# Expert results of a fused attention and mixture-of-experts kernel: scattered to their tokens as they come, and read back by plain loads

## What is computed

```python
x = L0_attn_x                                  # (2, 1024, 256): 2048 tokens of width 256
xn = layernorm(x)
# attention: (2, 1024, 256) seen as tokens of width 16, windows of 8 positions,
# softmax, a 3-tap convolution, projection, a norm over 16; result: "attention"
topk_idx, topk_weight = gate(xn)               # 6 of 16 experts for each token
out = 0
for e in range(16):
    inter = silu(xn @ gate_proj[e].T) * (xn @ up_proj[e].T)      # width 176
    out = out + comb[:, e:e+1] * (inter @ down_proj[e].T)        # comb: weight of e, or 0
shared = (silu(xn @ sg.T) * (xn @ su.T)) @ sd.T                  # width 352
return x + attention + out + shared
```

## Time and profile before

| what | us |
|---|---|
| three runs | 451.7, 457.14, 457.64 |
| median | 457.14 |
| the profiled execution, its time | 456.78 |
| its span, first to last instruction | 455.0 |

### The profile page before, as it was taken

The page is one execution under the profiler, slowest core; times in us unless marked ns, Lnnn a source line. Parts: engine busy times, 40 slices in busy tenths (PEclk is TensorE's granted clock), DMA queues, the critical chain, the costliest instruction groups (busy, mean ns, idle before and its releaser), DMA issues.

```text
span 455.0 us, 7300 instructions
## 1 busy us (share of the span) xinstructions
PE 400.8 (88%) x1989; PEld 310.2 (68%) x1989; DVE 364.8 (80%) x593; ACT 224.8 (49%) x616; POOL 234.7 (52%) x221
## 2 busy tenths in 40 slices
PE   7799599999999999997999999989989999999200
PEld 7688499889767677675777777767667777767200
DVE  2869953686899989999799999999995355479951
ACT  3654234325564445653476864675437744554200
POOL 3530156775777777873000000007787777778671
PEclk9889979999999999999899999999999999999755
DMA  7998422226455766576733334336657997665652
GB/s 169 330 412 354 163 107 88 98 76 223 132 184 190 205 207 197 184 229 184 216 114 103 97 95 121 103 90 169 196 166 202 287 234 194 175 198 160 201 151 81
DMA packets 55878, 80.55 MB, mean 177 GB/s; under 512 B 8480, under 2 KB 47264, under 8 KB 55584
## 3 DMA queue, kind: packets, MB, share of 16 engines
q1 hardware_dynamic: 42912, 50.91, 36.7%
q0 software_dynamic: 9216, 25.96, 18.8%
q10 hardware_dynamic: 3712, 3.21, 2.4%
HBM read 43.48 MB, written 36.57 MB: 176 GB/s over the span
## 4 chain that ended last, share of the span: by engine, by line
PE 49%; DVE 22%; issue 12%; DMA 5%; POOL 4%; ACT 2%; SPq 2%; ACTq 1%; DVEq 1%; POOLq 0%
PE gate L991 15%; PE ps_y L1014 10%; POOL xs_dram L594 4%; PE ps_y L942 4%; DVE prod L1094 4%; DVE qkv L1094 4%; PE up L920 3%; PE ps_y L1007 3%; DVE inter_s L1532 3%; PE up L981 3%; DVE sc L1094 2%; PE gate L920 2%; DVE yacc L1614 2%; PE misc L882 2%; PE misc L1041 2%
## 5 line engine op out<-in xcount | busy, mean ns | idle before, releaser
L991 PE MATMUL gate<-wrec,xgT 128*128 x444 | 151.3, 463 | 2.9 <-ACT xgT L725 1.8
L594 POOL DMA_INDIRECT xs_dram<-xrow,slot_i x96 | 111.4, 1160 | 50.6 <-DMA xs_dram<-xrow,slot_i 21.5
L1014 PE MATMUL ps_y<-wrec,interT 88*128 x444 | 115.2, 382 | 0.0
L614 POOL DMA_INDIRECT gat<-y_dram,slot_i x50 | 55.0, 1099 | 113.6 <-DMA y_dram<-y_s 98.9
L991 PEld LDWEIGHTS gate<-wrec,xgT 128*128 128x128 f32 x444 | 75.8, 190 | 28.2 <-issue 4.4
L1014 PEld LDWEIGHTS ps_y<-wrec,interT 88*128 88x128 f32 x444 | 76.0, 191 | 6.7 <-issue 0.3
L1532 DVE SCALAR_TENSOR_TENSOR inter_s<-gate,xg,gate_s 128x176 f32<-128x176 f32 x111 | 43.6, 393 | 33.8 <-ACT gate_s L733 32.9
L733 ACT ACTIVATE gate_s<-gate 128x176 f32<-128x176 f32 x111 | 35.2, 317 | 70.1 <-PE ps_y L1007 67.7
L753 ACT ACTIVATE y_s<-ps_y 128x256 f32<-128x256 f32 x107 | 41.0, 383 | 55.7 <-PE up L981 52.6
L1007 PEld LDWEIGHTS ps_y<-ident,inter_s 128*88 128x88 f32 x222 | 26.7, 123 | 37.6 <-issue 19.3
L1007 PE MATMUL ps_y<-ident,inter_s 128*88 128x128 f32 x222 | 42.7, 274 | 5.0 <-DVE y_s L1556 2.8
(11 more groups left out here) (215 smaller groups left out, 633.8 us busy)
## 6 DMA issues: line engine op xcount, KB each, us to landing
xg<-xs_dram SPq DMA_DIRECT2D x111, 136.0 KB, 2.6
y_dram<-y_s SPq DMA_DIRECT2D x111, 128.0 KB, 2.1
wrec<-wexp SPq DMA_DIRECT2D x14, 608.0 KB, 15.1
xs_dram<-zrow SPq DMA_DIRECT2D x1, 2176.0 KB, 13.0
xn_dram<-xrow SPq DMA_DIRECT2D x8, 256.0 KB
qkv<-xn_dram SPq DMA_DIRECT2D x8, 256.0 KB
xs_dram<-xrow,slot_i POOLq DMA_INDIRECT x96, 2.9
wrec<-wexp SPq DMA_DIRECT2D x1, 1216.0 KB, 5.6
```

The source lines that it names most:

```text
L594: nc.gpsimd.indirect_dma_start(xs_dram[0:DONE[max(d for d in DONE if d <= c)] * P, :], bass.IndirectOffsetOnAxis(slot_i[:, o:o + 1], 0), x ...
L614: nc.gpsimd.indirect_dma_start(places[place_of(n)][:, there:there + H], None, y_dram[0:DONE[max(d for d in DONE if d <= first)] * P, :], b ...
L991: last = nc.tensor.matmul(guA[t % 2][:, 0:2 * I], xgT[:, t % 2, k * P:(k + 1) * P], wrec[:, bass.ds(record + k * 2 * I, 2 * I)], start=(k ...
L1014: last = nc.tensor.matmul(ps_y[:, t % 2 * 2 * H:t % 2 * 2 * H + H], interT[:, t % 2, k * P:(k + 1) * P], wrec[0:HALF, bass.ds(record + KT ...
```

## The change

The gathers of the combine go; each tile's result rows are scattered to their tokens instead.

- Each dispatched row is 16 values wider (`XW` = 288): for each expert, the number of the row in `y_home` (2048 tokens x 6) that the product with that expert belongs to, token times 6 plus its rank among the six. `routing` computes it with two more VectorE operations. Rows of zero padding carry `NOWHERE` = 1e6 there.
- ScalarE copies, in each round, one column of the tile's table (the tile's expert) to `home_i` as integers (`home_rows`).
- SP stores the results of tiles 0 to 106 to `y_dram` as before, and loads each back to one of six buffers `y_back` in round max(38 + 5s//8, s + 4) (`load_back`); first it waits for the store and for the scatter that used the buffer before.
- POOL, after the dispatch, scatters tile s from there (tiles 107 to 110 directly from `y_s`) to `y_home`: 111 indirect DMAs, with a bounds check that drops the padding rows; for tile s it waits for `mid_ok` of at least 38 + 5s//8.
- SP loads fetch n from `y_home` with one plain DMA (rows of 1 KB, 6 KB apart), in rounds 84 to 90 one each, 91 to 101 three in two rounds, 104 to 106 two each, and the last twelve after the loop, at the head of its output stores; five places instead of seven. VectorE adds fetches 0 to 29 two rounds after their loads, 30 and 31 between the last steps of `normalise`, the rest at the end.
- `XN_AT` goes from 87 to 95 and `PACED` from 40 to 36. Some tables change places in SBUF.

```diff
-XW = H + NE
+XW = H + 2 * NE
+NOWHERE = 1e6
...
-PACED = 40
+PACED = 36
 YRING = 4
+HOME_FROM = 38
+YBACK = 6
+DIRECT = NT - YRING
...
-XN_AT = 87
+XN_AT = 95
...
-FEW, PLACES = 4, 7
+PLACES = 5
+READ_AT = {n: 84 + n if n < 7 else 91 + 2 * (n - 7) // 3 if n < 24 else 104 + (n - 24) // 2 for n in range(30)}
 ADD_AT = {}
-for _n in range(24):
-    ADD_AT.setdefault(76 + 14 * _n // 9, []).append(_n)
-def place_of(n):
-    return n % FEW if n < 2 * FEW else n % PLACES
-def before_at(n):
-    return next((m for m in range(n - 1, -1, -1) if place_of(m) == place_of(n)), None)
-def fetched(n):
-    return sum(last - first for first, last, _ in (FETCHES[m] for m in range(n + 1) if place_of(m) == place_of(n)))
+for _n, _t in READ_AT.items():
+    ADD_AT.setdefault(_t + 2, []).append(_n)
...
+def home_at(s):
+    return HOME_FROM + 5 * s // 8
+def back_at(s):
+    return max(home_at(s), s + 4)
+def read_at(n):
+    return READ_AT.get(n, NT + 3)
...
+        y_home = nc.dram_tensor("y_home", [T * TOP, H], F32).ap()
...
+        home_i = at("home_i", [P, RT], I32)
...
+        y_back = at("y_back", [P, YBACK, H])
+        gat = at("gat", [P, WIDE * H])
...
-            sp.wait_ge(zeros, 1)
+            sp.wait_ge(zeros, 2)
...
+            def load_back(s):
+                sp.wait_ge(put[s % YRING], 16 * (s // YRING + 1))
+                if s >= YBACK:
+                    sp.wait_ge(home[(s - YBACK) % LANES], 16 * ((s - YBACK) // LANES + 1))
+                sp.dma_start(y_back[:, s % YBACK, :], y_dram[s * P:(s + 1) * P, :]).then_inc(back[s % YBACK], 16)
+            by_token = y_home.rearrange("(c p k) w -> p c k w", p=P, k=TOP)
+            def load_results(n):
+                first, last, k = FETCHES[n]
+                landed(sp, home, DONE[max(d for d in DONE if d <= first)])
+                if n >= PLACES:
+                    sp.wait_ge(added, n - PLACES + 1)
+                else:
+                    sp.wait_ge(att_ok, 2 * B)
+                sp.dma_start(places[n % PLACES][:, 0:(last - first) * H].rearrange("p (c w) -> p c w", w=H), by_token[:, first:last, k, :]
+                             ).then_inc(got[n % PLACES], 16)
             for t in range(LEAD):
                 load_tile(t)
-            for t in range(NT + 3):
+            sent_back = read = 0
+            for t in range(NT + 4):
                 if t + LEAD < NT:
                     load_tile(t + LEAD)
-                if t >= 3:
+                if 3 <= t < DIRECT + 3:
                     store_tile(t - 3)
+                while sent_back < DIRECT and back_at(sent_back) <= t:
+                    load_back(sent_back)
+                    sent_back += 1
+                while read < len(FETCHES) and read_at(read) <= t:
+                    load_results(read)
+                    read += 1
...
+                if 3 <= t < DIRECT + 3:
...
-            nc.gpsimd.memset(zrow[:, :], 0.0).then_inc(zeros, 1)
+            nc.gpsimd.memset(zrow[:, 0:H + NE], 0.0).then_inc(zeros, 1)
+            nc.gpsimd.memset(zrow[:, H + NE:XW], NOWHERE).then_inc(zeros, 1)
...
-            def stored(c):
-                for i in range(YRING):
-                    pool.wait_ge(put[i], 16 * len(range(i, DONE[c], YRING)))
-            for n, (first, last, k) in enumerate(FETCHES):
-                if k == 0 and first in DONE:
-                    stored(first)
-                if before_at(n) is not None:
-                    pool.wait_ge(added, before_at(n) + 1)
-                elif n >= FEW:
-                    pool.wait_ge(att_ok, 2 * B)
-                for c in range(first, last):
-                    o, there = c * KEEP + k, (c - first) * H
-                    nc.gpsimd.indirect_dma_start(places[place_of(n)][:, there:there + H], None,
-                                                 y_dram[0:DONE[max(d for d in DONE if d <= first)] * P, :],
-                                                 bass.IndirectOffsetOnAxis(slot_i[:, o:o + 1], 0)).then_inc(got[place_of(n)], 16)
+            for s in range(NT):
+                pool.wait_ge(mid_ok, min(home_at(s), NT))
+                if s >= LANES:
+                    pool.wait_ge(home[s % LANES], 16 * (s // LANES))
+                if s < DIRECT:
+                    pool.wait_ge(back[s % YBACK], 16 * (s // YBACK + 1))
+                    rows = y_back[:, s % YBACK, :]
+                else:
+                    pool.wait_ge(y_sb, s + 1)
+                    rows = y_s[:, s % YRING, :]
+                nc.gpsimd.indirect_dma_start(y_home[:, :], bass.IndirectOffsetOnAxis(home_i[:, s:s + 1], 0), rows, None,
+                                             bounds_check=T * TOP - 1, oob_is_err=False).then_inc(home[s % LANES], 16)
...
+            def home_rows(t):
+                if t % 4 == 0:
+                    group = id_sets[t // 4 % 2]
+                    nc.scalar.load(group, e_row[0:1, t:t + 4])
+                    for i in range(4):
+                        id_at[t + i] = nc.scalar.snap(group[i], min_val=H, max_val=H + NE - 1)
+                nc.scalar.activation(home_i[:, t:t + 1], xg[:, t % RING, bass.ds(id_at[t] + NE, 1)], ACT.Copy)
...
+                if t + 1 < NT:
+                    home_rows(t + 1)
...
+                do(nc.vector.tensor_tensor_scan(area(VAL, 256), seg[:, :], chosen, 0.0, ALU.mult, ALU.add))
...
+                do(nc.vector.tensor_tensor(xw[:, :, H + NE:XW], ce(VAL), first_f[:, :].unsqueeze(2).to_broadcast([P, TOK, NE]), ALU.add))
...
-                dve.wait_ge(got[place_of(n)], 16 * fetched(n))
+                dve.wait_ge(got[n % PLACES], 16 * (n // PLACES + 1))
```

More of the change, by code:

```diff
@@ L225, in build @@
         mask8 = at("mask8", [P, WIN])
[L226 to L232, removed]
         slot_i = at("slot_i", [P, KEEP * TOK], I32)
@@ L253, in build @@
         zrow = at("zrow", [P, XW])
+        lane_f = at("lane_f", [P, 1])
+        stats = at("stats", [P, TOK, 6])
+        mv = at("mv", [P, TOK, 2])
+        rstd = at("rstd", [P, TOK])
+        expo = at("expo", [P, 8])
+        idle = at("idle", [P, 1])
+        first_f = at("first_f", [P, TOK])
         assert cursor[0] <= after_q, cursor[0] - after_q
@@ L291, in build @@
         lt = at("lt", [2 * NE, LTS, 2 * P], F32, sil_at)
+        gw = at("gw", [P, KT, 2 * NE], F32R)
         both = at("both", [2 * NE, NE])
@@ L315, in build @@
         got = [sem(f"got{i}") for i in range(PLACES)]
+        back = [sem(f"back{i}") for i in range(YBACK)]
+        home = [sem(f"home{i}") for i in range(LANES)]
         added = sem("added")
@@ L366, in by_lane @@
             return table[ROWS * b:ROWS * (b + 1), :].rearrange("(c r) w -> r c w", c=C)[r]
-        places = [gat[:, i, :] for i in range(FEW - 1)] + [spare[:, :], sc[:, 0:WIDE * H]] + [prod[:, i, H:H + WIDE * H] for i in range(2)]
+        places = [gat[:, :], spare[:, :], sc[:, 0:WIDE * H]] + [prod[:, i, H:H + WIDE * H] for i in range(2)]
         def bank(n):
@@ L518, in _ @@
             for i in range(YRING):
-                sp.wait_ge(put[i], 16 * len(range(i, NT, YRING)))
+                sp.wait_ge(put[i], 16 * len(range(i, DIRECT, YRING)))
         @block.gpsimd
@@ L568, in _ @@
                                     pattern=[[1, P]], channel_multiplier=-1).then_inc(tables, 1)
+            nc.gpsimd.iota(first_f[:, :], [[P * TOP, TOK]], base=-1, channel_multiplier=TOP,
+                           allow_small_or_imprecise_dtypes=True).then_inc(tables, 1)
             nc.gpsimd.memset(seg[:, :].rearrange("p (c e) -> p c e", e=NE)[:, :, 0:1], 0.0).then_inc(tables, 1)
@@ L676, in _ @@
             load_x(act, 0, 1)
-            act.wait_ge(zeros, 1)
+            act.wait_ge(zeros, 2)
             nc.scalar.activation(idle[:, :], zrow[:, 0:1], ACT.Sigmoid)
@@ L789, in late_step @@
                     nc.scalar.activation(xrow[:, j * 512:(j + 1) * 512], misc[j % 2][:, :], ACT.Square).then_inc(sq_ok, 1)
+            def home_rows(t):
[5 more added lines that the diff above has]
+                nc.scalar.activation(home_i[:, t:t + 1], xg[:, t % RING, bass.ds(id_at[t] + NE, 1)], ACT.Copy)
+            id_sets = [[act.alloc_register(f"id_of{s}_{i}") for i in range(4)] for s in range(2)]
+            id_at = {}
             act.wait_ge(qkv_ps, QKV_JOBS - WIN)
@@ L795, in _ @@
             columns(1)
+            act.wait_ge(xg_in[0], 16)
+            home_rows(0)
             for t in range(NT + 3):
@@ L1613, in add_results @@
                     dve.wait_ge(norm_ok, parts.value())
-                nc.vector.tensor_tensor(acc, acc, places[place_of(n)][:, 0:(last - first) * H], ALU.add).then_inc(added, 1)
+                nc.vector.tensor_tensor(acc, acc, places[n % PLACES][:, 0:(last - first) * H], ALU.add).then_inc(added, 1)
                 sums.add()
```

14 lines of the change are left out of this document (7 added, 7 removed).

## The result

The changed kernel takes **474.33 us** (median of 4 runs, 472.24 to 479.29), the kernel before 454.42 beside it: a ratio of 1.048 [1.034, 1.063]. Slower by 20 us, and above the range of 447 to 470. The profiled execution is the longest of the four: 479.29 us, span 477.6, against a span of 455.0 before.

What follows compares the result with a forecast made beforehand. Before the change PE and DVE were taken as full and DMA as idle capacity. 456.78 + 0.6 (early work) - 3.2 (rounds 76 to 84) + 5 (result loads) - 3.2 (tail) = 456.0 us, range 447 to 470.

Steps and rivals of the forecast that it cites:

- The DMA term: Result loads, rounds 84 to 104: 24.5 MB at 303 GB/s take 80.9 us, 13.3 too many; +5 us after cover.
- cover: Slack from early xg loads and additions two rounds after their loads, taken as 8 us of the 13.3 us excess.
- Rival R3: DMA at 274 GB/s, or PE waiting behind DVE's late load: +14 in place of +5, 465 us; chance 0.13.
- R1: Rival: DMA keeps up with the result loads, no stall, 451.0 us or down to 447.4; chance 0.30.
- Rounds 76 to 84: Six additions leave these rounds, so DVE keeps PE's pace of 2.49 us a round: -3.2 us.
- Scatter home: From round 38 results are stored, loaded back and scattered; POOL and DMA just keep up: 0 us.
- R2's throttle: Rival, rounds 38 to 94: scatters over 1.56 us hold up SP's loads back and the loop, 469 us; chance 0.12.
- The front: Two more DVE operations in routing delay the dispatch: +0.6 us; the new PACED number 0, up to 5.
- ScalarE's copies: 111 copies of 128x1 at 0.20 us, one a round, fit into ScalarE's free time: 0 us.
- The tail: After the last y_s copy: last scatters, loads, additions and SP's 20 output stores take 26.0 us against 29.2: -3.2 us.
- The sum: The profiled execution's 456.78 us plus all terms: 456.0 us, almost nothing gained.

Runs made afterwards that it cites:

- placing B: Sets of runs in which the kernel before takes 495 to 498 us; what makes a set fall there isn't known.
- c2: The changed kernel, unchanged, run again in the third set, in placing B: 491.9 us.
- c4: The changed kernel, unchanged, run again in set 5, in placing B; its median time isn't given.
- e10: The changed kernel without load back and scatter, result loads reading plain rows of y_dram: 467.1 us beside a before of 494.96.
- A: The placing, or sets of runs, in which the kernel before takes 454 us.
- e1: The changed kernel with SP loading each result back two rounds later: 476.32 us, ratio to the kernel before 1.058.
- e2: The changed kernel with result loads 5 to 23 bringing one column of three: 459.69 us, ratio 1.015.
- e3: The changed kernel with the normalised rows loaded eight rounds earlier (XN_AT 87 for 95): 472.06 us, ratio 1.047.
- e6: The changed kernel with results of tiles 90 to 106 scattered straight from SBUF, no store or load back: 480.94 us, before 497.63 beside it.
- e7: e6 with the normalised rows loaded eight rounds earlier (XN_AT 87 for 95): 488.2 us.
- e8: e6 with result loads later and closer together and the normalised rows four rounds earlier: 485.48 us, repeated at 486.65.
- e9: The changed kernel with additions three rounds behind their loads instead of two: 494.13 us beside a before of 497.63.

## Why the prediction was wrong

**The DMA term.** The counting was right: 24.5 MB by the prediction, 24.60 by the trace of after from 347.7 to 432.7 us. The DMA time was nearly right: 80.9 us at 303 GB/s were forecast, and the engines were busy for 0.94 of 85.0 us, 79.9. The step that failed is the next one: of the 13.3 us excess "I take 8 us" as cover. 17.4 us were lost, so on balance nothing was covered and 4.1 us more than the excess came on top. The two covers named are real: an xg load is asked for three rounds ahead and its landing may grow from 2.6 to 7.5 us, and an addition has two rounds. But they are a stock that is used up once, and by the same transfers: the first addition already had to wait 3.20 us for its load, up to 355.65, and PE waited 2.15 us for its tile, up to 356.49. The prediction also spread the bytes evenly over 67.6 us. At its 303 GB/s the three stretches would lose 3.6, 2.3 and 7.7 us; they lost 4.2, 0.0 and 13.2. The middle one did better than that rate, the last one, where the wide loads meet the normalised rows, far worse: 259 GB/s at a share of 0.92, with PE twice at half its clock. How much of that is the kind of transfer, how much the clock, no run separates. Rival R3 came nearest, DMA at 274 GB/s and +14, with a chance of 0.13; 17.4 lies beyond it too, and its other form, PE waiting for the product behind a late addition, doesn't appear in PE's waits.

R1 rested on there being room for 362 GB/s. The stage of after moved 289. Stretches of it moved more, with PE busy throughout:

```profile
368.00:388.00 20.00, 20.00 (x108) 14.70 (x106) 12.30 (x20) 10.79 (x35) 9.96 (x10) 1.00 1.02 346
```

The Trainium skill, "DMA: Bandwidth & Descriptors", section Specifications, has the HBM limit at about 358 GB/s a core. As a hard limit the traces don't bear it out: after in placing B moved 361 in 20 us (c2, 372 to 392 us) and 388 in 4 us (c4, 376 to 380). As the rate to plan with it gives an estimated 68 us where 85.0 were needed.

**Rounds 76 to 84.** Mechanism and size right: -3.2 forecast, -2.6 measured, -3.2 in e10. In B after's c4 gains 0.9 there, with ScalarE standing 1.6 us for something that the profile doesn't name.

**Scatter home.** Forecast 0, measured +2.1 in A. R2's throttle didn't come: a scatter didn't cost more than 1.56 us on average, bounds check included (1146 ns, and 0.3 of issue). Here is the new scatter's duration, min/median/max in ns, beside the dispatch's 954/962/2504:

```profile
L658 POOL DMA_INDIRECT y_home<-y_back,home_i x107: 982/985/2545, 229.8 to 449.1; - x107
```

SP waited only 7.5 us in all for the home semaphores up to 340 us. Most of the 2.1 us is lost in rounds 40 and 41, soon after the loads back begin; e1, e2 and e3 lose 1.6 to 3.7 in the stretch. In B after needs 10.4 us more there than in A (c4): ScalarE's unexplained waits are 7.2, and twice after them, at 273 and 314 us, PE's granted clock is at 0.50 for 3.4 us, an estimated 3.4 us of work in all.

**The front.** +0.6 forecast; e1 to e3 say -1.6 to +1.4. The 6.4 us of the profiled run are its own.

**ScalarE's copies.** 111 at 197 ns, as forecast (0.20); they show up in no stage of A.

**The tail.** From the last y_s copy 29.2 us before, 28.1 after; 26.0 forecast. Timeline, the tail of after:

```profile
449.05 2.54 POOL L658 DMA_INDIRECT y_home<-y_back,home_i  x1 [0.71 <-ACT y_s L796]
449.11 0.38 ACT L796 ACTIVATE y_s<-ps_y 128x256 f32<-128x256 f32 x1 [0.48 <-PE ps_y L1072]
...
457.20 1.11 POOL L658 DMA_INDIRECT y_home<-y_s,home_i  x1 [0.31 <-issue]
...
462.63 0.32 SPq L532 DMA_DIRECT2D spare<-y_home  x1
463.04 12.90 SPq L466 DMA_DIRECT2D out<-yacc  x20
...
465.35 0.42 DVE L1675 TENSOR_TENSOR yacc<-yacc,spare 128x256 f32<-128x256 f32 x1
```

With Y at 449.49 the last scatter starts at Y+7.7 where Y+3.3 was forecast: the first of the five starts 1.3 us later than worked out, and they were not 1.26 us apart but 1.3 to 2.9, since some run 1.4 to 2.5 us. From there the steps are as worked out: SP's 20 output stores start at Y+13.5 (9.6 forecast), take 12.90 us (12.6) and end 10.2 us after the last addition; 1.7 us follow (3.8). So the order of events was right; the scatters, taken at their usual length, came 4.4 us late, and the last landing gave 2.1 back.

**The sum.** With the front left aside, the profiled execution would be at 472.9: 456.78, plus 17.4, 2.1, less 2.6 and 0.8.

## What to carry over

Before work is moved onto a queue that seems idle, add up its bytes per stage and divide by the rate that the busiest mixed rows show; what comes out above the stage's time is a loss to count in full unless buffers are shown to cover it: here 8 us of cover were assumed and none remained. Do the sum per stretch and not per stage: where 324 GB/s were asked for nothing was lost, where 400 were, 4.2 and 13.2 us. Add that a PE that has waited may run on at half its clock, an estimated 5.1 us here. A way home through DRAM costs every byte three times (store, load back, scatter) before it is read; sparing the store and the load back for the last tiles (e6) gave 4 to 10 us against after, while no shift of the times at which things are loaded (e1, e3, e7, e8, e9) gave more than 2.3. A chain that runs through a queue's waits shows where transfers stand, and only an edit that removes the wait (e1) shows whether the wait was the cause.

## What the runs showed of the hardware

- At a share of 1.00 to 1.11 the DMA engines moved between 237 (e10, 408 to 412 us) and 388 GB/s (c4, 376 to 380 us) in windows of 4 us, in after with nearly all packets under 2 KB: share 1 is no fixed rate. It reached 1.11 with SP's queue alone, POOL idle (e10, 396 to 400 us).
- After PE had waited 2.15, 2.56 and 2.22 us for tiles, its granted clock fell from 1.00 to 0.50 for 3.4 us each time (after).
- An indirect scatter of 128 rows of 1 KB with a bounds check takes POOL 985 ns in the median, one of 128 rows of 1.1 KB without it 962; the two differ in more than the check.
- The kernel before took 454 us in two sets of runs and 495 to 498 in four, and in the one trace of it taken there ScalarE stands up to 9.8 us at a time for something that the profile doesn't name. A change of 5% could not have been judged across the sets; each needs the kernel before beside it.
